# Lower parts of x on GpSimd, first values and first queries at new places in a fused adapter, attention and FFN kernel

## The reference, cut to what matters

```python
c = x @ W.T + b + 2.0 * (x @ lora_A[slot]) @ lora_B[slot]   # per batch, x is 8 x 256 x 1024
q, k, v = c @ w_q, c @ w_k, c @ w_v                         # 32 query heads, 8 key and value heads, head size 32
o = softmax(q @ k.T / sqrt(32)) @ v
x = x + o @ w_o
x = x + 4.0 * topk_gated_lora(x @ cond2_weight[slot2].T)    # top 2 of 4 experts, rank 16
```

## Time and profile before

| what | us |
|---|---|
| profiled execution, its own time | 1028.63 |
| its span | 1027.0 |
| median of the 3 runs | 1028.95 |
| TensorE matmuls busy | 998.8 (97%) |
| TensorE weight loads busy | 806.7 (79%) |
| VectorE busy | 640.3 (62%) |
| ScalarE busy | 447.1 (44%) |
| GpSimd busy | 234.5 (23%) |
| ScalarE's idle time at L474, ended by DMA of x_raw | 42.3 in 14 waits |

### The profile page before, as it was taken

How to read it: one execution, slowest core, us unless ns; L and a number is a source line. 1 busy time by engine, 2 the same in 40 slices (tenths; PEclk the granted TensorE clock), 3 DMA queues, 4 the chain that set the end, 5 groups by cost and what they waited for, 6 DMA issues and landing times.

```text
span 1027.0 us, 17259 instructions
## 1 busy us (share of the span) xinstructions
PE 998.8 (97%) x6822; PEld 806.7 (79%) x6822; DVE 640.3 (62%) x1101; ACT 447.1 (44%) x786; POOL 234.5 (23%) x224
## 2 busy tenths in 40 slices
PE   7999999999999999999999999999999999999996
PEld 6878788777687776877767777785888889889886
DVE  6571722777846877467776588766655555655653
ACT  5121222356635657446655567746331332322321
POOL 1000001043323333224332246745110110011100
PEclk9999999999999999999999999999999999999998
DMA  7030411111411214111223424255866756766531
GB/s 269 0 103 1 134 54 48 42 44 38 125 46 38 59 44 126 36 42 49 54 90 89 111 78 133 79 160 204 259 210 198 230 190 202 243 191 190 196 124 41
DMA packets 49887, 117.40 MB, mean 114 GB/s; under 512 B 7298, under 2 KB 26114, under 8 KB 45712
## 3 DMA queue, kind: packets, MB, share of 16 engines
q1 hardware_dynamic: 40080, 81.70, 26.6%
q0 software_dynamic: 9728, 34.61, 10.7%
HBM read 86.38 MB, written 18.89 MB: 103 GB/s over the span
## 4 chain that ended last, share of the span: by engine, by line
PE 89%; DVE 4%; DMA 3%; ACT 1%; SPq 1%; issue 1%; POOL 0%; POOLq 0%; ACTq 0%
PE psP L818 20%; PE psW L1137 17%; PE psF L280 12%; PE psG L1165 8%; PE psO L909 5%; PE psS L885 5%; PE psT L896 5%; PE psX L1388 3%; PE psO L913 2%; PE psY L1407 2%; PE psF L291 2%; PE psP L840 2%; DVE nmax L734 1%; DMA x_raw<-in_xT 1%; DVE q_stack L703 1%; PE psP L842 1%
## 5 line engine op out<-in xcount | busy, mean ns | idle before, releaser
L596 POOL TENSOR_TENSOR p_sum<-probs 128x512 f32<-128x512 f32 x128 | 168.8, 1320 | 348.9 <-ACT probs L645 348.8
L818 PE MATMUL psP<-x_hl,wq 128*128 128x512 f32 x960 | 239.9, 395 | 0.2 <-DVE v_sb L724 0.2
L734 DVE TENSOR_REDUCE nmax<-psS 128x2 f32<-128x512 f32 x256 | 164.3, 683 | 103.8 <-PE psS L885 99.9
L818 PEld LDWEIGHTS psP<-x_hl,wq 128*128 128x128 f32 x960 | 175.5, 190 | 32.1 <-DVE v_sb L724 0.4
L1137 PE MATMUL psW<-wq 128*128 128x256 f32 x1536 | 196.9, 284 | 0.0
L1137 PEld LDWEIGHTS psW<-wq 128*128 128x128 f32 x1536 | 190.6, 191 | 4.0
L645 ACT ACTIVATE probs<-psT 128x512 f32<-128x512 f32 x256 | 139.0, 595 | 61.7 <-PE psT L896 60.8
L1146 ACT ACTIVATE cond_hi<-cond_raw 128x1024 fp32r<-128x1024 f32 x64 | 66.8, 1057 | 150.1 <-PE psG L1165 146.0
L1150 DVE TENSOR_TENSOR cond_lo<-cond_raw,cond_hi 128x1024 fp32r<-128x1024 f32 x64 | 78.7, 1240 | 82.1 <-ACT cond_hi L1146 82.1
L703 DVE TENSOR_TENSOR q_stack<-psP,q_stack 32x512 fp32r<-32x512 f32 x128 | 87.8, 686 | 9.1 <-ACT q_stack L610 7.1
L885 PEld LDWEIGHTS psS<-k_stack,q_stack 96*128 96x128 f32 x512 | 78.9, 189 | 17.5 <-issue 2.9
(11 more groups left out here) (128 smaller groups left out, 1295.1 us busy)
## 6 DMA issues: line engine op xcount, KB each, us to landing
cond_raw<-in_cond POOLq DMA_DIRECT2D x64, 512.0 KB, 4.0
x_raw<-in_xT SPq DMA_DIRECT2D x32, 256.0 KB, 3.2
q_stack<-q_stack SPq DMA_DIRECT2D x32, 256.0 KB, 2.9
o_scratch<-o_sb SPq DMA_DIRECT2D x64, 128.0 KB
o_raw<-rden_scratch SPq DMA_DIRECT2D x32, 256.0 KB, 5.0
o_raw<-o_scratch SPq DMA_DIRECT2D x8, 1024.0 KB, 8.9
x_sb<-in_xT SPq DMA_DIRECT2D x8, 1024.0 KB, 6.6
outT<-x_sb SPq DMA_DIRECT2D x32, 256.0 KB, 2.5
```

The lines of the kernel that those rows point to most:

```text
L596: pool.tensor_tensor(p_sum[:, heads], probs[:, 0, heads], probs[:, 1, heads], ALU.add).then_inc(sum_done, 1)
L734: dve.tensor_reduce(nmax[:, n % 2, 2 * hp:2 * hp + 2, qt], psS[:, i % 2].rearrange("p (h k) -> p h k", h=2), AX.X, ALU.max, negate=True).t ...
L818: mm = pe.matmul(out, wq[:, i, w, k * P:(k + 1) * P], x[:, k, part], start=(k == 0 and n_ == 0), stop=False)
```

## The change

In the three places where a pair's projections meet the next pair's (pairs 0 to 2), five things are placed anew:

- ScalarE rounds x tiles 0 to 3 in step 10, between the copied output and the exponentials of parts 2 and 3, and no longer at the end of step 9.
- The low parts of tiles 0 to 4 move from VectorE (steps 10 and 11) to GpSimd: tiles 0 to 2 behind the two sums that it makes during step 10, tiles 3 and 4 behind the two sums of step 11. They count in a new semaphore `x_lo_early`. Tiles 5 to 7 stay on VectorE.
- TensorE does tiles 0 and 1 of v0 in step 11's second slice, which was empty, and tiles 2 and 3 in step 12's first slice, where all four were.
- TensorE waits for the low part of each tile by a new function, `x_split`, which picks the semaphore.
- ScalarE copies the next pair's first query block q0 at the head of step 15, ahead of the maxima's rows, the exponentials and the copied output of that step.

```diff
-    (["q7:5-8"], []),
-    (["+v0:0-4"], ["+v1:0-4"]),
+    (["q7:5-8"], ["+v0:0-2"]),
+    (["+v0:2-4"], ["+v1:0-4"]),
...
-X_HI = {(9, 1): range(4), (11, 0): [4], (12, 0): [5, 6], (12, 1): [7]}
-X_LO = {(10, 0): range(4), (11, 1): [4], (12, 1): [5, 6], (13, 0): [7]}
+X_HI = {(10, 0): range(4), (11, 0): [4], (12, 0): [5, 6], (12, 1): [7]}
+X_LO = {(12, 1): [5, 6], (13, 0): [7]}
+X_LO_POOL = {10: range(3), 11: [3, 4]}
+XP = 5
...
+    def split_x_lo(engine, p, k, done):
+        engine.wait_ge(x_hi_done, KT * p + k + 1)
+        engine.tensor_tensor(x[:, k, 1], x_raw[:, k, 1], f(x[:, k, 0]), ALU.subtract).then_inc(done, 1)
+
+    def x_split(pe, p, k):
+
+        if p == 0:
+            pe.wait_ge(x_lo_done, k + 1)
+        elif k < XP:
+            pe.wait_ge(x_lo_early, XP * (p - 1) + k + 1)
+        else:
+            pe.wait_ge(x_lo_done, KT + (KT - XP) * (p - 1) + k - XP + 1)
...
                 pool.tensor_tensor(p_sum[:, heads], probs[:, 0, heads], probs[:, 1, heads], ALU.add).then_inc(sum_done, 1)
+            if p + 1 < PAIRS:
+                for k in X_LO_POOL.get(s + 2, ()):
+                    split_x_lo(pool, p + 1, k, x_lo_early)
             ahead.gpsimd(pool, n + 2)
...
             for unit_ in soon(n, 0):
-                if unit_[1][0] == "v":
+                if unit_[1][0] == "v" or unit_[1] == "q0":
                     evacuate(*unit_)
...
             for unit_ in soon(n, 0):
-                if unit_[1][0] != "v":
+                if unit_[1][0] != "v" and unit_[1] != "q0":
                     evacuate(*unit_)
...
-                    pe.wait_ge(x_lo_done, KT * p + k + 1)
+                    x_split(pe, p, k)
```

More of the change, by code:

```diff
@@ L407, in attend_stage @@
     x_hi_done, x_lo_done, x_used = sem("x_hi_done"), sem("x_lo_done"), sem("x_used")
+    x_lo_early = sem("x_lo_early")
     a_landed, a_hi_done, a_lo_done = sem("a_landed"), sem("a_hi_done"), sem("a_lo_done")
@@ L474, in split_x_hi @@
         nc.scalar.activation(x[:, k, 0], x_raw[:, k, 1], ACT.Copy).then_inc(x_hi_done, 1)
-    def split_x_lo(dve, p, k):
-        dve.wait_ge(x_hi_done, KT * p + k + 1)
-        dve.tensor_tensor(x[:, k, 1], x_raw[:, k, 1], f(x[:, k, 0]), ALU.subtract).then_inc(x_lo_done, 1)
+    def split_x_lo(engine, p, k, done):
[8 more added lines that the diff above has]
+            pe.wait_ge(x_lo_done, KT + (KT - XP) * (p - 1) + k - XP + 1)
     def split_a_hi(act, p):
@@ L505, in ahead_vector @@
         for k in [KT - 1] if last else range(KT - 1):
-            split_x_lo(dve, 0, k)
+            split_x_lo(dve, 0, k, x_lo_done)
         if not last:
@@ L752, in step @@
                 for k in X_LO.get((s, 0), ()):
-                    split_x_lo(dve, p + 1, k)
+                    split_x_lo(dve, p + 1, k, x_lo_done)
             for unit_ in late(n - 1) if n else [(0, "q1")]:
```

## The result

| | before | after |
|---|---|---|
| median of 11 runs, us | 1028.19 (1025.31 to 1031.06) | 1031.96 (1028.76 to 1033.28) |
| profiled execution, us | 1028.63 | 1033.28 |
| its span, us | 1027.0 | 1030.7 |
| mean granted clock | 0.992 | 0.989 |

The ratio is 1.0033, with a 95% interval from 1.0018 to 1.0047: the changed kernel is slower by about 0.3%, some 3.4 us. The forecast was 1031.2, the median is 1031.96. A second sample of the same kernel, among the experiments, gave 1.0038 (1.0019 to 1.0058).

What follows compares the result with a forecast made beforehand. TensorE, busy 97% of the span, was taken to bound the kernel, so only its waits and clock count. Waits 0.0, clock +4.5, q0 -1.8 give +2.7 on 1028.63, 1031.3, stated as 1031.2; own range 1029 to 1033.5.

Steps and rivals of the forecast that it cites:

- Step 10 and the sums' matmuls: Step 10 on TensorE: the sums' matmuls wait for GpSimd's sum, step ends at 7.15 us, 0.6 worse than clean.
- v0's first tiles: Step 11: TensorE waits 1.0 us for v0's bank, until 9.2 us after step 10's small transpose starts (T).
- Tile 3 behind GpSimd's queue: Step 12: v0's tile 3 waits 3.1 us for its low part, queued on GpSimd behind two sums, until T+14.4.
- the delay of 0.2 by VectorE: GpSimd's low parts ahead of tile 3: VectorE's small operations come between and get 0.2 us.
- v1 at T+17.4: Step 12: v1 starts there without its old wait; against before +1.4, -0.6 and -1.1 us in pairs 0 to 2.
- Rival 1: Low parts on GpSimd are hidden: v1 at about T+15.4, -8 us in all, some 1021; chance 0.10.
- The clock: Low clock once per place after TensorE's waits, 1.5 us each: +4.5 us; bounds 0 and 3.0 per place.
- rival 3: The clock falls twice at each place, another 1.5 us in three places: 1035.8; chance 0.23.
- rival 2: The waits come as worked out but TensorE's clock stays up, no 4.5 us: 1026.8; chance 0.17.
- q0: Step 15: the next pair's first scores lose their wait for q0, 0.6 us in three places: -1.8 us.
- The sum: All places together: 0.0 for the waits, +4.5 clock, -1.8 q0, so +2.7 us on the profiled 1028.63.
- The chances: For the median against a 0.3% border: faster 0.15, same 0.45, slower 0.40; the forecast itself 0.50.

Runs made afterwards that it cites:

- mid3: The changed kernel with x tiles 0 to 3 rounded behind step 10's exponentials and low parts of tiles 3 and 4 on VectorE; median 1024.04, ratio 0.9967 to before.
- lo3_front: The changed kernel with tile 3's low part on GpSimd ahead of step 11's sums; median 1028.66 us, ratio 1.0016 to the kernel before.
- v0_old: The changed kernel with all four tiles of v0 back in step 12's first slice; median 1027.92 us, ratio 1.0023 to the kernel before.
- lo3_dve: The changed kernel with the low parts of tiles 3 and 4 back on VectorE; median 1028.43 us, ratio 1.0004 to the kernel before.
- all_dve: The changed kernel with every low part of x on VectorE, GpSimd making only its sums; median 1023.79 us, ratio 0.9968 to the kernel before.
- after_again: The changed kernel run once more without an edit; median 1032.47 us, ratio 1.0038 to the kernel before.
- first four experiments: q0_alone, lo3_dve, v0_old and all_dve, 12 runs each, beside 35 runs of the kernel before with median 1026.64 us.
- last four: after_again, lo3_front, dve_old and mid3, 12 runs each, beside 35 runs of the kernel before with median 1027.87 us.
- q0_alone: The kernel before with only the early copy of q0 at the head of step 15; median 1025.71 us, ratio 0.9981 to the kernel before.
- dve_old: The changed kernel with every low part of x on VectorE and v0's tiles in their old place; median 1028.91 us, ratio 0.9998 to the kernel before.

## Why the prediction came out right

**Step 10 and the sums' matmuls: right.** 7.15 us was forecast from the clean step and the row of GpSimd's sum, and 7.15 was measured in all three pairs, with 0.28 us of wait at L928. Where the exponentials go ahead of the four roundings, as in mid3, the step is 6.55.

**v0's first tiles: right, a little dear.** A wait of 1.0 us until T+9.2 was forecast; it is 0.74 us, until T+9.12, since TensorE arrived 0.2 later. The transposed scores of step 11 are where they were put, at T+9.95.

**Tile 3 behind GpSimd's queue: right.** T+14.4 was forecast after 3.1 us of wait; it is T+14.08 after 2.5. A low part takes 1.25 us where I took 1.27, and the delay of 0.2 by VectorE did not come. It went the other way: VectorE was the one held.

**v1 at T+17.4: right in place (17.15), but for half of the reason.** I took q7's low parts as done by T+17.1 with one locked-out rounding in it, and they were done at T+16.85 with two. So tile 3's wait moved v1 by 0.3 us at most; without it, in lo3_front, v1 is 0.23 us earlier. The rule of the Trainium skill that the prediction named (SBUF — State Buffer, Who interferes with whom) says that the operation that comes second is blocked for the whole of the other; the traces agree, with 1.15 and 1.26 us where 0.17 is the free price. The 4.85 us of v0_old, over four operations of GpSimd, go beyond what that rule says. L757, with two inputs in SBUF, is held like the cast. L718 and L749, which take an input from PSUM, keep their 0.70 and 0.64 us per operation beside a working GpSimd.

**Rival 1 was mis-sized.** It gave T+15.4 and 1021 us were tile 3 in time. lo3_front makes just that true, and v1 is at 16.92: the low parts ahead of step 11's sums push both sums, one right behind the other, onto VectorE's two small operations, and these are locked out twice. For v1 at 15.9 one of the two lock-outs has to go (lo3_dve, pairs 0 and 1), and even with none of the low parts on GpSimd it is 16.15 (all_dve), since VectorE then does more itself.

**The clock: the term of the sum that was mis-sized.** Once per place and 1.5 us each made 4.5. In the first profile it fell in two of three places, at some 1.6 us each (24.28 and 24.35 against 22.72): 3.2. In the second it stayed low longer in two: 5.5. The two are around 4.5, but neither is three times 1.5. It fell twice in no place, as rival 3 had it, and stayed up, as rival 2 had it, in two of the six. The kernel before has such losses too, at 1.2 GHz after ScalarE's wait for x; they were in the measured sums that I compared with, so nothing was counted twice. But since those are 3.0 us (1.58 and 1.40), the forecast of +2.7 really said 1.5 us more loss by the clock and 1.2 us more of everything else.

**q0: right.** -0.62, -0.61 and -0.54 us in the three places against -0.6 each, and about -2.0 us by the experiment alone.

**The sum.** From T10 to T16, the six steps that hold all of it, after less before is +0.57, +0.45 and -0.25 us in the first profiles, +0.8 in all, where +2.7 was forecast; in after_again it is +3.1 (63.52, 61.12 and 63.47 against 60.17, 62.20 and 62.62). The medians say +3.8 and +4.6. I can't assign the rest to a place, about 3 us against the first profiles and 1 against after_again: the clock's falls differ from one execution to the next, and a profile is one execution. The chances had 0.40 on slower by over 0.3%, and the ratio stands just at that border.

**Near the number, in part by luck.** For the runs below the mean granted clock of each is known. The share of the clock that is missing, times the span, is an estimate of what the clock cost the run. Means, in us:

| kernel | runs | lost to the clock | span without that |
|---|---|---|---|
| before, beside the first four experiments | 35 | 6.5 | 1018.7 |
| before, beside the last four | 35 | 7.4 | 1018.6 |
| q0_alone | 12 | 6.7 | 1016.8 |
| after | 11 | 10.7 | 1019.0 |
| after_again | 12 | 11.1 | 1019.2 |
| all_dve | 12 | 5.5 | 1016.7 |

q0_alone comes out with 1.8 to 1.9 us less work and the clock of before, as forecast. after has 0.3 to 0.6 us more work than before, and 3.3 to 4.6 us more loss by the clock. The forecast, read in this way, had 1.2 and 1.5. So the slowdown is nearly all clock; the clock's term was too small by 2 to 3 us and the rest too large by some 0.8 (v1 at 17.15 and not 17.4, three times), and the two errors offset each other in part. The estimate is rough: it also counts a low clock while TensorE waits anyway. At which places of the span the runs without a profile lost it isn't shown.

**Where the 3 to 4 us come from, by the experiments.** Read as a chain of ratios: the first queries early, 0.9981; the roundings of x moved on top of it with all low parts on VectorE, 0.9998 (dve_old); v0's tiles early on top of that, 0.9968 (all_dve); five low parts to GpSimd on top of that, 1.0033 and 1.0038. Each ratio is known to some 1.5 to 2.6 us, so a single step of the chain is no surer than 2 to 3 us. The last step costs about 7 us. Of these 3.1 are direct, 22.72 against 21.68 in a place with the clock up. The other 4 I put down to the clock: in all_dve's trace it doesn't fall in these three places, in the two traces of after it fell in four of six. The table of all runs agrees, with 5.2 to 5.6 us of the clock and 2.3 to 2.5 of the rest. That the waits of 2.5 us are what brings it down isn't shown: the clock stayed up behind such waits in two of six places and behind one of 2.35 us (lo3_dve, pair 2), and fell in all three places of lo3_front behind 1.14.

## What to carry to other kernels

Work that goes from a full engine to an idle one still stands in that engine's queue: put down what is due behind it (here tile 3 behind two sums), and the time of the shared port with VectorE, before calling it free. When several places of a kernel do the same work, compare their traces with each other first; a difference between them is wait and clock. One profile against another can put the difference in a place that the change doesn't touch; the medians and a second profile of the same kernel tell whether it belongs there. The mean granted clock of every run, not only of the profiled one, separates what the clock cost from what the work cost.

## What the runs showed of the hardware that I had not expected

A 128x8 rounding on VectorE was held over four GpSimd operations in a row (4.85 us), while in other places with the same queue it got in after the first (1.12 to 1.15 us). Which of the two happens was not settled. The free price is 0.17 us. In after it takes 0.69 at 263.11 and ends at 263.80, as the sum that GpSimd started at 262.47 (1.30 us) does; so even where it looked like a plain price it was a wait.

The low clock behind waits of the same length (2.51 to 2.55 us) lasted some 3.4 us, some 6.8 us, or didn't come. The 12 times of lo3_dve, from 1021.67 to 1033.43 us, are in three groups some 5 us apart, each with its own mean granted clock.
